# Two expert outputs per token joined to the residual by accumulating DMAs

## The chip, the cores and the metric

The kernel runs on one core of a Trainium2 chip. The metric is device time in microseconds for one execution. A core has five engines with queues of their own: PE (TensorE, matrix products), VectorE (DVE), ScalarE (ACT), GpSimd (POOL) and SyncE (SP), and 16 DMA engines which they share. Instructions of one queue run in order; between queues only semaphores order the work. A DMA raises its semaphore by 16 when all of its data has landed.

## What is computed

A model of two layers over 4 x 512 tokens of width 128. In layer 0 a gated recurrence and a mixture of 8 experts both read the normalised input and are added to it. The mixture picks two experts for each token and adds their weighted outputs:

```python
out = out * scores.reshape(-1, 1)
combined = out.reshape(N, TOP_K, h).sum(axis=1)      # TOP_K = 2
...
x = x + _L0_attn_ref(xn, ...) + _L0_ffn_ref(xn, ...)
xn = _layernorm(x, axis=-1)
x = x + _L1_attn_ref(xn, ...) + _L1_ffn_ref(xn, ...)
```

Layer 1 normalises the sum again and feeds a state-space scan and a mixture of 64 experts. Nothing of layer 1 can start before the sum of layer 0 is complete. The change is at this join.

## The kernel before

Tokens lie 128 to a tile, 16 tiles (NT), in 4 blocks (NB) of 4 tiles (TPB). The residual `res` is in SBUF as [128, 16, 128] float32: partition p, tile c holds token 128 c + p. It is loaded at L396.

Layer 0's experts work on tokens sorted by expert, in 39 tiles (NTILE) of 128 rows. In a loop over these tiles (PE from L1399, ScalarE from L729, VectorE from L1098, POOL from L530) a tile's rows are gathered from DRAM by an indirect DMA of POOL (`fetch`, L497), go through the expert and are scattered by another indirect DMA (`send`, L509) into the DRAM tensor `parts`. Each row of `parts` is one token's output of one of its two experts, 512 bytes, already weighted. Behind a padding area the rows lie by token, then by expert: row 2 t + k is expert k of token t. The attention's output is added to `res` on VectorE (L1081), one block at a time, within the same loop; the semaphore `back_dve` counts that chain.

The join comes after the loop:

- SP waits for the last of `back_dve` (L430) and for all scatters (`o_sent`, L432), then loads `parts` into the SBUF tensor `both` with four DMAs, one a block (L435). Each has its own semaphore `both_in[b]`. A token's two rows are adjacent, so a row of a transfer is 1 KB.
- VectorE (from L1109) waits for a block, adds both outputs to `res` (L1113, two instructions of 128 x 512), and takes the statistics for the normalisation (L1115 bn_stats, L1119 bn_aggr, four each). After the last block it forms the variance (L842), ScalarE takes the root (L754), VectorE inverts it (L1124) and normalises 16 tiles into `xn_tok` (L1126). PE transposes these (L1256), and layer 1 goes on from there.
- POOL, after its last scatter, splits the weights of the first two expert groups of layer 1 into high and low parts (`split_group`: L477, L478, L538), raises `g_split`, and then waits for ScalarE's exponentials (L546). PE uses these parts from L1486 and L1490 on.
- SP, after the loads, enters a loop that waits for `g_split` and reloads `g_raw` (L388) for the next two groups.

Layer 1 has accumulating DMAs of its own: POOL issues them at L572 and adds `state`, 512 KB with 4 KB in each partition, to `y_t` (the memory of `xn_tok`), both in SBUF.

Of the kernel before, what the change touches and what calls it, by code (L numbers as in the profile page):

```python
# [6 lines left out]
ALU = mybir.AluOpType  # L7
# [6 lines left out]
P = 128  # L14
# [24 lines left out]
def program(nc, x, wq, wk, wv, wa, wg, wo, rms_scale, wqkv, w1, w2, A_log, B_mat, C_mat, D_vec, W_dt, b_dt,  # L39
# [9 lines left out]
    NB, T, D = x.shape  # L49
    NTOK = NB * T  # L50
    NT = NTOK // P
    TPB = TB // P
    E0, F2, _ = w1.shape
    F = F2 // 2
    FT = [(s, min(P, F - s)) for s in range(0, F, P)]
    NF = len(FT)
    E1, _, H1 = rw1.shape
    GE = P // H1
    NG = E1 // GE
    NS = A_log.shape[1]  # L60
    ES, _, HS = sw1.shape
    NSH = ES * HS // P
    LN_EPS, RMS_EPS = 1e-5, 1e-6
    TOPK = 2
    NTILE = NTOK * TOPK // P + E0 - 1
    XRING, ORING, TRING, AHEAD = 12, 4, 3, 10
# [11 lines left out]
    parts = nc.dram_tensor("parts", (NTOK * TOPK + NTILE * P, D), F32).ap()  # L78

    with ExitStack() as ctx:  # L80
        def sb(name, shape, dt=F32):
            return ctx.enter_context(nc.sbuf_tensor(name, shape, dt))

        def sem(name):
            return ctx.enter_context(nc.semaphore(name))
# [25 lines left out]
        def over(base, limit):  # L111

            offset = base

            def place(name, shape, dt=F32):
                nonlocal offset
                t = nc.alloc_sbuf_tensor_at(name, shape, dt, offset=offset)
                offset += (math.prod(shape[1:]) * 4 + 31) // 32 * 32
                assert offset <= limit, (name, offset, limit)
                return t  # L120

            return place

        res = sb("res", [P, NT, P])
# [23 lines left out]
        both = over(base, nc.sbuf_base)("both", [P, NT, TOPK, P])  # L148
# [122 lines left out]
        h0_made, sil_ready, gated, h_turned = sem("h0_made"), sem("sil_ready"), sem("gated"), sem("h_turned")  # L271
        h_copied, o_made, o_out = sem("h_copied"), sem("o_made"), sem("o_out")
        o_sent = [sem(f"o_sent{r}") for r in range(ORING)]
        both_in = [sem(f"both_in{b}") for b in range(NB)]
        fr_pe, fr_act, fr_dve = sem("fr_pe"), sem("fr_act"), sem("fr_dve")
        back_pe, back_act, back_dve = sem("back_pe"), sem("back_act"), sem("back_dve")
        dt_made, dt_left, sp_exp, sp_log = sem("dt_made"), sem("dt_left"), sem("sp_exp"), sem("sp_log")
# [30 lines left out]
        def counted(steps, ops):  # L308

            table, total = {}, 0  # L310
            for name, b in steps:
                total += ops[name]
                table[name, b] = total
            return table
# [29 lines left out]
        def beside(n, names):  # L344

            return [(name, b) for b, first in enumerate(BACK_AT) for name in names if first + BACK_STEPS[name] == n]

        BK_DVE = counted([what for n in range(NTILE + 3) for what in beside(n, BACK_OPS)], BACK_OPS)
# [23 lines left out]
        def _(sp):  # L372
# [54 lines left out]
            sp.wait_ge(fr_dve, max(FR_DVE.values()))  # L427
            sp.dma_start(sw1_raw[:, :, :], sw1.rearrange("e d h -> d e h")).then_inc(late_in, 16)
            sp.dma_start(sw2_sb[:, :, :], sw2.rearrange("e (c h) d -> h (e c) d", h=P)).then_inc(late_in, 16)
            sp.wait_ge(back_dve, max(BK_DVE.values()))  # L430
            for r in range(ORING):
                sp.wait_ge(o_sent[r], 16 * ((NTILE - 1 - r) // ORING + 1))  # L432
            parts_v = parts[NTILE * P:NTILE * P + NTOK * TOPK, :].rearrange("(c p k) d -> p c (k d)", p=P, k=TOPK)
            for b in range(NB):
                sp.dma_start(both[:, b * TPB:(b + 1) * TPB, :, :].rearrange("p c k d -> p c (k d)"),  # L435
                             parts_v[:, b * TPB:(b + 1) * TPB, :]).then_inc(both_in[b], 16)
            with sp.Fori(0, NG // GPI - 1) as i:
                for j in range(GPI):

# [14 lines left out]
        def _(pool):  # L454
            own = Chain(pool, pool_own)
# [37 lines left out]
            def fetch(n):  # L493

                if n >= XRING:
                    pool.wait_ge(x_turned, n - XRING + 1)
                pool.indirect_dma_start(  # L497
                    out=x_tile[n % XRING][:, :], out_offset=None, in_=normed,
                    in_offset=bass.IndirectOffsetOnAxis(ap=token[:, n:n + 1], axis=0)).then_inc(x_tile_in[n % XRING], 16)
# [6 lines left out]
            def send(n):  # L506

                pool.wait_ge(o_out, n + 1)
                pool.indirect_dma_start(  # L509
                    out=parts, out_offset=bass.IndirectOffsetOnAxis(ap=part[:, n:n + 1], axis=0),  # L510
                    in_=t_out[n % ORING][:, :], in_offset=None).then_inc(o_sent[n % ORING], 16)

            def prepare(n):

                sel_v = sel[:, :].rearrange("p (c h) -> p c h", h=H1)
                if n == 27:
                    pool.wait_ge(late_in, 16 * 8)
                    split(rout_raw[:, :], rout_hi[:, :], rout_lo[:, :])
                    own(pool.tensor_tensor(ssm_cb[:, :], ssm_raw[:, 1, :], ssm_raw[:, 2, :], ALU.mult))
                if n == 29:  # L520
                    split(sw1_raw[:, :, :], sw1_hi[:, :, :], sw1_lo[:, :, :])
                    pool.nop().then_inc(weights_split, 1)
                if n == 31:
                    own(pool.memset(sel[:, :], 0.0))
                if n in (33, 35):
                    own(pool.affine_select(out=sel_v, in_=sel_v, compare_op=ALU.not_equal, fill=1.0,
                                           base=-E1 * ((n - 33) // 2), pattern=[[-1, E1], [0, H1]],
                                           channel_multiplier=1))

            for n in range(NTILE):  # L530
                send(n)
                prepare(n)
                if n + AHEAD < NTILE:
                    fetch(n + AHEAD)

            def split_group(j):
                split(g_raw1[j][:, :, :].rearrange("p e h -> p (e h)"), g_hi[j][:, :], g_lo[j][:, :])
                own(pool.tensor_copy(sel_now[j][:, :], sel[:, j * P:(j + 1) * P]))  # L538
                pool.nop().then_inc(g_split, 1)
# [10 lines left out]
            for b in range(POOL_LOGS):  # L550
                pool.wait_ge(sp_exp, b + 1)
                e, _, p = softplus_bufs[b]
                own(pool.tensor_scalar(p[:, :], e[:, :], -1.0 / 4, 1.0 / 3, ALU.mult, ALU.add))
                own(pool.tensor_tensor(p[:, :], p[:, :], e[:, :], ALU.mult))
                own(pool.tensor_scalar(p[:, :], p[:, :], 1.0, -1.0 / 2, ALU.mult, ALU.add))
                own(pool.tensor_tensor(p[:, :], p[:, :], e[:, :], ALU.mult))
                own(pool.tensor_scalar(p[:, :], p[:, :], 1.0, 1.0, ALU.mult, ALU.add))
                own(pool.tensor_tensor(p[:, :], p[:, :], e[:, :], ALU.mult))
                pool.nop().then_inc(sp_poly, 1)
# [268 lines left out]
        def _(dve):  # L828
            own = Chain(dve, dve_own)
# [52 lines left out]
            q, k, v = (qkv[:, :, n * E0:(n + 1) * E0] for n in range(3))  # L882
# [224 lines left out]

            dve.wait_ge(back_dve, max(BK_DVE.values()))
            for b in range(NBLK):  # L1109
                dve.wait_ge(both_in[b], 16)  # L1110
                r = res[:, b * TPB:(b + 1) * TPB, :]
                for k in range(TOPK):
                    own(dve.tensor_tensor(r, r, both[:, b * TPB:(b + 1) * TPB, k, :], ALU.add))  # L1113
                for t in range(b * TPB, (b + 1) * TPB):
                    dve.bn_stats(stats[:, t, :], res[:, t, :]).then_inc(dve_own, 1)  # L1115
                own.n += TPB
                own.wait()
                for t in range(b * TPB, (b + 1) * TPB):
                    dve.bn_aggr(mv[:, t, :], stats[:, t, :]).then_inc(dve_own, 1)  # L1119
                own.n += TPB  # L1120
# [65 lines left out]
            def poly(b):  # L1186

                e, _, p = softplus_bufs[b]
                dve.wait_ge(sp_exp, b + 1)
                own(dve.tensor_scalar(p[:, :], e[:, :], -1.0 / 4, None, ALU.mult))  # L1190
                for c in (1.0 / 3, -1.0 / 2, 1.0):
                    own(dve.scalar_tensor_tensor(p[:, :], p[:, :], c, e[:, :], ALU.add, ALU.mult))
# [31 lines left out]
            for i in range(NG // GPI):  # L1224
                c = i * GSTEPS
# [13 lines left out]
            for b in range(NBLK):  # L1239
                dve.wait_ge(sum_turned, b + 1)  # L1240
                r = res[:, b * TPB:(b + 1) * TPB, :].rearrange("p t d -> p (t d)")
# [306 lines left out]
```

## Time and profile before

| | us |
|---|---|
| median of 3 runs | 472.01 (471.5 to 472.09) |
| profiled execution | 475.62 |
| span of the profiled execution, first to last instruction | 473.9 |

| engine | busy us | share of the span |
|---|---|---|
| PE | 346.5 | 73% |
| VectorE | 347.8 | 73% |
| ScalarE | 261.5 | 55% |
| GpSimd | 243.2 | 51% |

Times in the rows are from the start of the span. A busy share is an average over stages with different limits, so the page is read together with the chain that ended last. That chain goes back from the last instruction, at each step to what released it. The join lies between 232 and 253 us.

### The profile page before, as it was taken

To read this page: it belongs to the slowest core of one execution; us is meant where nothing else is said; L and a number is where in the kernel's file an instruction comes from. 1 tells how busy PE (TensorE), PEld (TensorE's weight loads), DVE (VectorE), ACT (ScalarE), POOL (GpSimd) and SP (SyncE) were. 2 spreads that over 40 slices of the span, in tenths; PEclk is the share of its full clock that TensorE was granted. 3 is DMA by queue.
4 is the path that set the end of the run, shared out by engine and by line. 5 is a ranking of instruction groups with operands and counts; after the bars stand their busy time and mean duration, and the time that the engine had idled before them with its cause. 6 is when DMAs were issued, how large, how long until landed. Compare 5 with 4: busy or idle time off the path is not lost.

```text
span 473.9 us, 5780 instructions
## 1 busy us (share of the span) xinstructions
PE 346.5 (73%) x1491; PEld 247.2 (52%) x1491; DVE 347.8 (73%) x615; ACT 261.5 (55%) x440; POOL 243.2 (51%) x254
## 2 busy tenths in 40 slices
PE   1846879667975987779506848977887887887883
PEld 0435659356854866668403524544554554554542
DVE  5679998897864866648169759908688688688674
ACT  1477654546458346374505675355856856856820
POOL 3475300704763676776800049005577877877850
PEclk9977675959997898998956975997999999999997
DMA  6374100100111112120160000004658658668574
GB/s 175 94 200 128 25 1 1 45 11 24 46 39 29 34 41 81 43 42 21 35 190 0 0 0 2 0 0 89 126 101 161 123 116 163 122 119 162 112 152 111
DMA packets 36213, 35.09 MB, mean 74 GB/s; under 512 B 12166, under 2 KB 30839, under 8 KB 36183
## 3 DMA queue, kind: packets, MB, share of 16 engines
q0 software_dynamic: 7104, 21.90, 22.7%
q1 hardware_dynamic: 29078, 12.84, 10.2%
q8 instruction: 14, 0.23, 0.2%
q14 instruction: 17, 0.13, 0.1%
HBM read 13.29 MB, written 4.65 MB: 38 GB/s over the span
## 4 chain that ended last, share of the span: by engine, by line
PE 35%; POOL 19%; DVE 19%; issue 13%; ACT 6%; DMA 3%; another core or an unknown queue 2%; DVEq 1%; SPq 0%; POOLq 0%; ACTq 0%
POOL state L568 10%; PE psum L1376 5%; POOL xn_tok L572 4%; PE psum L1349 4%; POOL g_hi L581 3%; PE psum L1365 3%; PE psum L1389 3%; PE psum L1443 3%; PE psum L292 3%; PE psum L293 2%; PE psum L294 2%; PE psum L1352 2%; PE psum L1355 2%; PE psum L1338 1%
## 5 line engine op out<-in xcount | busy, mean ns | idle before, releaser
L1212 DVE TENSOR_TENSOR_SCAN state<-dec,win_t 128x1024 f32<-128x1024 f32 x32 | 73.4, 2293 | 26.5 <-ACT dec L777 26.5
L568 POOL TENSOR_SCALAR state<-state,ssm_cb 128x1024 f32<-128x1024 f32 x32 | 49.7, 1553 | 48.0 <-DVE state L1212 45.0
L812 ACT ACTIVATE sil<-psum,vec_t 128x512 f32<-128x512 f32 x64 | 43.2, 687 | 48.3 <-PE psum L294 37.7
L509 POOL DMA_INDIRECT parts<-t_out,part x39 | 41.0, 1050 | 48.3 <-ACT t_out L726 41.9
L1498 PE MATMUL psum<-hid,g_w 128*128 128x512 f32 x128 | 62.1, 599 | 0.0
L1221 DVE TENSOR_TENSOR hid<-sil,psum 128x512 f32<-128x512 f32 x64 | 41.7, 676 | 12.9 <-ACT sil L812 10.9
L497 POOL DMA_INDIRECT x_tile<-normed,token x39 | 41.3, 1059 | 13.4 <-issue 10.7
L292 PE MATMUL psum<-xn_hi,g_hi 128*128 128x512 f32 x64 | 39.7, 620 | 11.3 <-ACT sil L812 11.3
L1094 DVE TENSOR_TENSOR t_hid<-t_sil,psum 128x352 f32<-128x352 f32 x39 | 20.3, 521 | 32.3 <-ACT t_sil L710 23.5
L717 ACT ACTIVATE t_hid_t<-psum 128x384 f32<-128x384 f32 x39 | 19.2, 492 | 38.9 <-PE psum L1365 25.3
L1376 PE MATMUL psum<-w_out,t_hid_t 128*128 x234 | 37.5, 300 | 2.2 <-ACT t_out L726 1.4
L1490 PE MATMUL psum<-cw_hl,sel_now 128*128 128x512 f32 x64 | 26.9, 420 | 14.9 <-DVE hid L1221 14.9
L1376 PEld LDWEIGHTS psum<-w_out,t_hid_t 128*128 128x128 f32 x234 | 31.6, 205 | 5.3 <-issue 4.2
L572 POOL DMA_DIRECT2D xn_tok<-state x32 | 28.8, 899 | 10.2 <-POOL state L568 9.6
L1349 PE MATMUL psum<-w_hi,xt_hi 128*128 x78 | 25.1, 406 | 11.8 <-issue 11.8
L1498 PEld LDWEIGHTS psum<-hid,g_w 128*128 128x128 f32 x128 | 24.5, 191 | 15.0 <-issue 11.5
L777 ACT ACTIVATE dec<-dt_t,ssm_a 128x2044 f32<-128x2044 f32 x16 | 31.1, 1992 | 0.1
L292 PEld LDWEIGHTS psum<-xn_hi,g_hi 128*128 128x128 f32 x64 | 12.5, 195 | 26.4 <-ACT sil L812 19.3
L1338 PE MATMUL psum<-ident,x_tile 128*128 128x128 f32 x39 | 12.1, 310 | 18.8 <-DVE xt_lo L1086 13.7
L294 PE MATMUL psum<-xn_lo,g_hi 128*128 128x512 f32 x64 | 25.7, 402 | 0.0
L293 PE MATMUL psum<-xn_hi,g_lo 128*128 128x512 f32 x64 | 25.7, 402 | 0.0
L1490 PEld LDWEIGHTS psum<-cw_hl,sel_now 128*128 128x128 f32 x64 | 12.3, 193 | 22.3 <-DVE hid L1221 20.1
(308 smaller groups left out, 887.6 us busy)
## 6 DMA issues: line engine op xcount, KB each, us to landing
xn_tok<-state POOLq DMA_DIRECT2D x32, 512.0 KB, 4.5
e_raw<-in_L_ffn_w SPq DMA_DIRECT2D x16, 128.0 KB, 2.2
both<-parts SPq DMA_DIRECT2D x4, 512.0 KB, 5.6
e_raw<-in_L_ffn_w SPq DMA_DIRECT2D x8, 176.0 KB, 2.6
res<-in_L_attn_x SPq DMA_DIRECT2D x4, 256.0 KB, 3.8
normed<-rows SPq DMA_DIRECT2D x1, 1024.0 KB, 5.2
g_raw<-in_L_ffn_w SPq DMA_DIRECT2D x16, 64.0 KB, 2.3
g_w<-in_L_ffn_w SPq DMA_DIRECT2D x16, 64.0 KB, 2.2
```

Source lines behind the costliest of these rows:

```text
L292: pe.matmul(acc, w_hi, m_hi, start=True, stop=False)
L497: pool.indirect_dma_start(out=x_tile[n % XRING][:, :], out_offset=None, in_=normed, in_offset=bass.IndirectOffsetOnAxis(ap=token[:, n:n + ...
L509: pool.indirect_dma_start(out=parts, out_offset=bass.IndirectOffsetOnAxis(ap=part[:, n:n + 1], axis=0), in_=t_out[n % ORING][:, :], in_off ...
L568: own(pool.tensor_scalar(state[k][:, :], state[k][:, :], ssm_cb[:, i * GPI + k // 2:i * GPI + k // 2 + 1], 0.0, ALU.mult, ALU.add))
L572: pool.dma_start(y_t[:, (k % 2) * HALF:(k % 2 + 1) * HALF], state[k][:, :], accum_op=ALU.add).then_inc(y_in[k], 16)
L812: act.activation(sil[:, c % 2, :], ps[c % 2][:, :], ACT.Silu, bias=vec_t[:, V_B1 + c // NBLK:V_B1 + c // NBLK + 1]).then_inc(h_silu, 1)
L1212: dve.tensor_tensor_scan(state[k][:, :], dec[n % DECS][:, at_half], win_t[:, at_half], 0.0, ALU.mult, ALU.add).then_inc(scanned, 1)
L1221: dve.tensor_tensor(hid_ring[c % HRING], sil[:, c % 2, :], ps[2 + c % 2][:, :], ALU.mult).then_inc(hid_done, 1)
L1349: pe.matmul(acc[c], xt_hi[n % TRING][:, :], w_hi[:, e, half[c]].rearrange("p a f -> p (a f)"), start=True, stop=False)
L1376: ins = pe.matmul(ps[O_BANK][:, 0:P], t_hid_t[n % 2][:, c * P:(c + 1) * P], w_out[:, e, c, :].rearrange("p a d -> p (a d)"), start=(c == 0 ...
L1490: pe.matmul(ps[2 + c % 2][:, :], sel_now[j][:, :], blk(cw_hl, tb), start=True, stop=True).then_inc(cwx_made, 1)
L1498: pe.matmul(ps[4 + tb][:, :], g_w2[g % GPI][:, :], hid_ring[c % HRING], start=False, stop=g == NG - 1, skip_group_check=True).then_inc(g_o ...
```

## The change

The four loads of SP, the tensor `both` as their target and the eight additions of VectorE go. In their place POOL, after its last scatter, issues four DMAs that add into `res` as they write: first expert 0 for the first and the second half of the tiles, then expert 1 for each half. An expert 1 DMA waits until the expert 0 DMA of its half has landed. VectorE waits for both DMAs of the half in which a block lies, and takes the statistics.

```diff
--- before.py
+++ after.py
@@ -271,7 +271,7 @@
         h0_made, sil_ready, gated, h_turned = sem("h0_made"), sem("sil_ready"), sem("gated"), sem("h_turned")
         h_copied, o_made, o_out = sem("h_copied"), sem("o_made"), sem("o_out")
         o_sent = [sem(f"o_sent{r}") for r in range(ORING)]
-        both_in = [sem(f"both_in{b}") for b in range(NB)]
+        both_in = [sem(f"both_in{h}") for h in range(2)]
         fr_pe, fr_act, fr_dve = sem("fr_pe"), sem("fr_act"), sem("fr_dve")
         back_pe, back_act, back_dve = sem("back_pe"), sem("back_act"), sem("back_dve")
         dt_made, dt_left, sp_exp, sp_log = sem("dt_made"), sem("dt_left"), sem("sp_exp"), sem("sp_log")
@@ -427,13 +427,6 @@
             sp.wait_ge(fr_dve, max(FR_DVE.values()))
             sp.dma_start(sw1_raw[:, :, :], sw1.rearrange("e d h -> d e h")).then_inc(late_in, 16)
             sp.dma_start(sw2_sb[:, :, :], sw2.rearrange("e (c h) d -> h (e c) d", h=P)).then_inc(late_in, 16)
-            sp.wait_ge(back_dve, max(BK_DVE.values()))
-            for r in range(ORING):
-                sp.wait_ge(o_sent[r], 16 * ((NTILE - 1 - r) // ORING + 1))
-            parts_v = parts[NTILE * P:NTILE * P + NTOK * TOPK, :].rearrange("(c p k) d -> p c (k d)", p=P, k=TOPK)
-            for b in range(NB):
-                sp.dma_start(both[:, b * TPB:(b + 1) * TPB, :, :].rearrange("p c k d -> p c (k d)"),
-                             parts_v[:, b * TPB:(b + 1) * TPB, :]).then_inc(both_in[b], 16)
             with sp.Fori(0, NG // GPI - 1) as i:
                 for j in range(GPI):
 
@@ -533,6 +526,18 @@
                 if n + AHEAD < NTILE:
                     fetch(n + AHEAD)
 
+            pool.wait_ge(back_dve, max(BK_DVE.values()))
+            for r in range(ORING):
+                pool.wait_ge(o_sent[r], 16 * ((NTILE - 1 - r) // ORING + 1))
+            parts_v = parts[NTILE * P:NTILE * P + NTOK * TOPK, :].rearrange("(c p k) d -> p c k d", p=P, k=TOPK)
+            for k in range(TOPK):
+                for h in range(2):
+                    at_half = slice(h * NT // 2, (h + 1) * NT // 2)
+                    if k > 0:
+                        pool.wait_ge(both_in[h], 16 * k)
+                    pool.dma_start(res[:, at_half, :], parts_v[:, at_half, k, :], accum_op=ALU.add
+                                   ).then_inc(both_in[h], 16)
+
             def split_group(j):
                 split(g_raw1[j][:, :, :].rearrange("p e h -> p (e h)"), g_hi[j][:, :], g_lo[j][:, :])
                 own(pool.tensor_copy(sel_now[j][:, :], sel[:, j * P:(j + 1) * P]))
@@ -1107,10 +1112,7 @@
 
             dve.wait_ge(back_dve, max(BK_DVE.values()))
             for b in range(NBLK):
-                dve.wait_ge(both_in[b], 16)
-                r = res[:, b * TPB:(b + 1) * TPB, :]
-                for k in range(TOPK):
-                    own(dve.tensor_tensor(r, r, both[:, b * TPB:(b + 1) * TPB, k, :], ALU.add))
+                dve.wait_ge(both_in[b // 2], 16 * TOPK)
                 for t in range(b * TPB, (b + 1) * TPB):
                     dve.bn_stats(stats[:, t, :], res[:, t, :]).then_inc(dve_own, 1)
                 own.n += TPB
```

## Rows read from the trace of the kernel before

**Rows 1.** The page, part 4: shares of the span in the chain that ended last.

```profile
PE 35%; POOL 19%; DVE 19%; issue 13%; ACT 6%; DMA 3%; another core or an unknown queue 2%; DVEq 1%; SPq 0%; POOLq 0%; ACTq 0%
```

**Rows 2.** The chain in order of time at the join: start, us, what.

```profile
234.73 2.24 DMA parts<-t_out,part
...
237.13 3.98 DMA both<-parts
...
241.20 0.70 DVE res L1113
241.93 0.70 DVE res L1113
242.65 0.88 DVE stats L1115 x4
243.56 0.38 DVE mv L1119 x4
...
250.52 0.88 DVE stats L1115 x4
251.43 0.39 DVE mv L1119 x4
...
252.74 4.19 DVE xn_tok L1126 x16
```

**Rows 3.** Groups of instructions, 234 to 253 us: busy us, mean ns | idle before.

```profile
L1113 DVE TENSOR_TENSOR res<-res,both 128x512 f32<-128x512 f32 x8 | 5.4, 680 | 12.1 <-DMA both<-parts 12.0
L1115 DVE BATCH_NORM_STATS2 stats<-res 128x6 f32<-128x128 f32 x16 | 3.5, 280 | 0.1
...
L1119 DVE BATCH_NORM_AGGREGATE mv<-stats 128x2 f32<-128x6 f32 x16 | 1.5, 157 | 0.1
```

**Rows 4.** Line 435, the loads; then windows: start:end, us, five engines, clock, DMA, GB/s.

```profile
L435 SPq DMA_DIRECT2D both<-parts x4: 359/432/510, 237.1 to 238.9; - x4
...
DMA to landing us min/median/max: 4.0/5.6/7.3
...
2.50:5.50 3.00, 0.00 (x0) 0.00 (x0) 1.50 (x8) 0.00 (x0) 2.43 (x8) 1.00 1.02 288
...
242.50:244.00 1.50, 0.00 (x0) 0.00 (x0) 1.43 (x10) 0.00 (x0) 0.00 (x0) 0.50 1.07 366
```

**Rows 5.** Line 572, layer 1's accumulating DMAs: ns min/median/max; and a window of one.

```profile
L572 POOL DMA_DIRECT2D xn_tok<-state x32: 890/896/1002, 324.1 to 459.4; - x32
...
DMA to landing us min/median/max: 4.5/4.5/5.3
...
425.10:427.70 2.60, 2.60 (x7) 1.14 (x6) 1.68 (x1) 2.60 (x2) 2.30 (x3) 1.00 1.04 202
```

**Rows 6.** Timeline of POOL from the last scatter: start, us, instruction, idle before.

```profile
234.73 0.97 POOL L509 DMA_INDIRECT parts<-t_out,part  x1 [0.30 <-issue]
235.73 0.30 POOL L477 TENSOR_SCALAR g_hi<-g_raw 128x128 fp32r<-128x128 f32 x1
...
238.02 0.29 POOL L538 CAST sel_now<-sel 128x128 fp32r<-128x128 bf16 x1
```

**Rows 7.** Windows around the join: PE, PEld, DVE, ACT, POOL busy; clock; DMA share; GB/s.

```profile
237.00:241.00 4.00, 0.00 (x0) 0.00 (x0) 0.00 (x0) 0.00 (x0) 1.04 (x3) 0.50 0.67 203
...
253.00:257.00 4.00, 3.85 (x15) 2.74 (x16) 4.00 (x17) 3.44 (x7) 0.00 (x0) 0.50 0.00 0
257.00:261.00 4.00, 3.71 (x17) 1.82 (x17) 3.58 (x6) 2.07 (x4) 0.00 (x0) 0.96 0.00 0
```

**Rows 8.** Lines 1081, 1490, 583 (first and last start) and a wait of POOL.

```profile
L1081 DVE TENSOR_TENSOR res<-res,psum x4: 677/678/680, 130.7 to 226.2; 128x512 f32<-128x512 f32 x4
...
L1490 PEld LDWEIGHTS psum<-cw_hl,sel_now x64: 186/188/330, 314.8 to 457.0; 128*128 128x128 f32 x64
...
L583 POOL CAST sel_now<-sel x14: 289/291/291, 330.1 to 446.7; 128x128 fp32r<-128x128 bf16 x14
...
278.32 0.43 POOL L549 MEMSET dec<- 128x4 f32 x3 [40.01 <-ACTq L793]
```

## The prediction

> **What bounds the kernel now.** I read the page's share of the chain first. No engine owns this kernel: PE has 35% of the chain that ended last, POOL and VectorE 19% each [rows 1]. So totals of busy time say nothing here, and a change is worth what it does to the chain at its place. The next view is the same chain in order of time around that place [rows 2]. The last scatter of an expert output is issued at 234.73 and lands 2.24 us later. SP, released, issues the load of both at 237.13; the first quarter lands after 3.98 us. From 241.20 the chain stays on VectorE: two additions of 0.70 us, four statistics, four aggregates, four times over, until 251.8; then the root, and from 252.74 the 16 normalising instructions from which the whole second layer starts. Nothing else is on the way: the stretch is serial, and PE idles through it [rows 7]. A microsecond gained or lost before 251.8 moves the end of the kernel by a microsecond.
>
> The groups of that stretch [rows 3] say what VectorE does in it: eight additions, 5.4 us, and statistics and aggregates of 3.5 and 1.5 us. In the chain a block takes 2.65 us (10.6 / 4), of which 1.45 are its additions (241.20 to 242.65, [rows 2]); 1.2 us are left, and two blocks take 2.5.
>
> The stretch thus is: 237.1 to 241.2 for the transfer, 10.6 us of VectorE, end at 251.8. Of the four loads only the first shows; the other three land beneath the additions (to landing 4.0 to 7.3 us, the last issued at 238.9, [rows 4]).
>
> **Part 1: removed.** Four SP loads and eight additions. The additions are worth 5.4 us on the chain, and the first load 4.1 us. That is all there is to win: 9.5 us, out of which the new transfers have to be paid.
>
> **Part 2: added.** Four accumulating DMAs on POOL's queue, each half of the tokens (512 KB) and one of the two experts. POOL is ready for the first at about 237.2: the same landing at 236.97, which was SP's to wait for, and 0.3 us, the gap that POOL shows ahead of a DMA [rows 6]. Call D the time that POOL spends issuing one, and d the time that the DMA engines spend on the data of one.
>
> The nearest row is the accumulating DMA of the second layer, state into xn_tok: the same 512 KB, float32, SBUF to SBUF. It occupies POOL for 0.89 us and lands 4.5 us after its start [rows 5]. In a stretch where almost only one of them moves, the engines are full (share 1.04) and carry 202 GB/s [rows 5]: 524 KB in 2.6 us. So 4.5 = 0.9 of issue + 2.6 of data + 1.0 of start and completion. Two plain loads give the scale: with 1 KB rows full engines carry 366 GB/s, with 512 B rows 288 [rows 4]. An accumulation thus costs almost twice a copy.
>
> Two things differ from that row, and both come from the shape: parts is interleaved, so each DMA has 8 x 128 = 1024 rows of 512 B where state has 128 rows of 4 KB.
>
> d: the lower end is 2.6 us (row length free). Upper: if the loss from small rows counts for both the read and the add, 2.6 x (366/288) squared = 4.2, an estimate. I take one factor of 366/288, 3.3 us, since only one of the two sources has short rows by necessity. A gain is excluded only if an accumulation from HBM is no faster than one from SBUF; what it would be otherwise is rival A.
>
> D: lower end 0.9 us, the row. Upper end: if POOL's time is all per row, 8 x 0.9 = 7.2 us. Which? The scatter moves 128 rows of 512 B with an index for each and takes 0.97 us; the accumulation has an extra source for each of its 128 rows and takes 0.89 [rows 5, 6]. A second source that costs nothing visible speaks for a price that is mostly fixed. If half is per row, D is 4.0; if a fifth, 2.2. I take 2.5, nearer to the row.
>
> **The sum.** The order is k0 half 0, k0 half 1, k1 half 0, k1 half 1; a k1 is issued when its own k0 has landed. All share the same engines, so once they are fed the data are back to back: while D is under d, the next one is issued beneath the data of the one before. VectorE now needs both halves of the experts before a half's statistics; the first half's 2.5 us lie beneath the last transfer, the last half's 2.5 do not, and 0.1 is the release.
> End = 237.2 + D + 1.0 + 4 d + 2.6.
> With D = 2.5, d = 3.3: 237.2 + 2.5 + 1.0 + 13.2 + 2.6 = 256.5, against 251.8: 4.7 us later. With both lower ends (0.9, 2.6): 252.1, 0.3 us later. So even where the shape costs nothing, four accumulations one after the other (10.4 us of data) use up what the 5.4 us of additions and the overlapped loads gave. Break-even is D + 4 d = 11.0.
>
> The profiled execution took 475.6 us for a span of 473.9 and the median is 472.0; I add the difference to the median: 472.0 + 4.7 = 476.7.
>
> A price from the Trainium skill stands against this. *DMA: Bandwidth & Descriptors*, section "Anatomy of one DMA — SWDGE (gpsimd) path", gives a DMA issued from GpSimd as 2.0 us plus bytes over 436 GB/s, 3.2 us for 512 KB, where the row of this trace shows 4.5. The same section says that many descriptors can be generated before the cost of more shows. By that sentence D would be 0.9 and the sum 237.2 + 0.9 + 1.0 + 13.2 + 2.6 = 254.9, 3.1 us later; no row of this trace shows a DMA of POOL with more than 128 rows.
>
> **Part 3: moved.** SP's wait for back_dve goes to POOL: the last addition of the attention's output is done by 227 [rows 8], no cost. Both expert groups' splits (six instructions, 2.1 us, 235.73 to 238.3 [rows 6]) now stand behind the four DMAs on POOL, including two waits for landings, so they run at about 253 to 256. Who needs them: PE's first load of sel_now at 314.8 [rows 8], and SP's two reloads of g_raw, issued now after them, for a use at 330. POOL's own next work waits until 278 for the exponentials [rows 8]. The cover is at least 22 us, and it moves with the chain; cost nothing. If POOL's issues took all of the upper end they would end before 267, still covered. The reloads, which stood behind the four loads on SP's queue, no longer meet them.
>
> PE's clock: from 237 to 257 PE is granted 0.50, that is 1.2 GHz, having done nothing since 233; the next four microseconds show 0.96 [rows 7]. It works from 253.1 and is at 2.4 GHz by 257 to 261. A longer idle time leaves the same state at its end, so the slow stretch shifts and costs nothing more.
>
> **Rivals.**
> A, faster: an accumulation from HBM runs at the rate of a plain load. For: one source is HBM and no longer the SBUF; the two reads might overlap. Against: the row of 202 GB/s at full engines. Price: d = 524/288 = 1.8. k0 half 0 lands at 240.9, k1 half 0 is issued at 241.2 and lands 3.7 later, 244.9; its k1 half 1 follows within 2 us, and both statistics run from 244.9 to 249.9: 1.9 us earlier, 470.1. It decides from about d = 2.5, 210 GB/s. By the skill's 3.2 us for each DMA the same chain would end at 249.0, 469.2; this trace speaks against it with 4.5.
>
> B, issue bound: POOL pays per row and D passes d. Then the end is 237.2 + 4 D + 1.0 + d + 2.6. D = 4: 8.3 later, 480.3. D = 5: 264.1, 12.3 later, 484.3. D = 7.2: 272.9, 493. For: every DMA of POOL here has 128 rows, so nothing bounds the slope. Against: the scatter and accumulation pair above.
>
> C, small rows weigh on an accumulation more than on a copy, since each then stands for two reads and a write: d = 4.6, an estimate between the second and the third power of 366/288 (4.2 and 5.3). D = 2.5: 237.2 + 2.5 + 1.0 + 18.4 + 2.6 = 261.7, 9.9 later, 481.9.
>
> E, nothing: the ends meet, the result within 0.9 us. For: both lower ends give +0.3.
>
> **How the numbers follow.** The forecast (D from 0.9 to 3.7, d from 2.6 to 3.6) has 0.50 and an own range of 473 to 480; A 0.13; B 0.17; C 0.12; E 0.08. A difference of 0.2%, 0.9 us, is about what can be told from none. Faster by more: A, 0.13. Same: E and a sliver of the forecast, 0.12. Slower: 0.75. The range goes from 470.9, which takes in a part of A, to 487, which takes in C and B up to D = 5.7; outside stay most of A and the top of B, under 0.2.
>
> **What would show it.** In the changed kernel the four DMAs' own rows: their time on POOL (D: 2.5 forecast, 0.9 the row, over 4 is B), the spacing of their landings, the GB/s at full engines (160 forecast, 202 the row, 290 is A, under 120 is C). VectorE's wait before the first statistics should end near 250.6 (253.9 less 3.3), and the last half's near 254. The normalising instructions should start near 257.4. From there to the end, both traces should run in step; if POOL's splits or g_raw's reloads show as a releaser of anything, part 3 is wrong. The prediction is wrong if D + 4 d is under 11 or the issue is the longer of the two.

## The result and the profile after

The changed kernel takes 476.73 us (median of 5 runs, 476.42 to 480.08) where the kernel before takes 472.09 (471.5 to 475.7). The ratio is 1.0086, 95% interval 1.0044 to 1.0128: slower by 4.1 us, clear of no change. Measured once more beside the experiments, it was 1.0116 (1.0068 to 1.0164). The forecast was 4.7 us.

| | before | after |
|---|---|---|
| profiled execution | 475.62 us | 480.08 us |
| its span | 473.9 us | 478.3 us |
| VectorE busy | 347.8 us | 341.8 us |
| GpSimd busy | 243.2 us | 251.0 us |

The engine that the change relieves is busy for 6 us less, and the kernel is slower. The page shows what the DMA engines got in exchange: the same 35.09 MB in over 2000 packets more. The packets of POOL's queue, q0, take 26.0% of the engines' span where they took 22.7%.

```profile
span 478.3 us, 5772 instructions
DMA packets 38260, 35.09 MB, mean 73 GB/s; under 512 B 12165, under 2 KB 32886, under 8 KB 38230
q0 software_dynamic: 11264, 23.99, 26.0%
```

The chain in order of time at the join, to be laid beside [rows 2] (start, us, what):

```profile
235.91 2.23 DMA parts<-t_out,part
...
238.84 1.00 POOL res L538
239.84 8.53 DMA res<-parts
...
248.65 6.99 DMA res<-parts
...
255.66 0.89 DVE stats L1117 x4
256.57 0.38 DVE mv L1121 x4
256.95 0.77 DVE stats L1117 x4
257.74 0.39 DVE mv L1121 x4
...
258.25 0.19 DVE nrm L847
```

Where the chain before had one short transfer and then VectorE's work, it now has 17 us from POOL's first issue to the last landing, and VectorE has only the tail. The measure that I use from here on is the stretch from the landing of the last scatter to the start of the variance (L842, now L847). Before it is 236.97 to 251.94, 15.0 us; after, 238.14 to 258.25, 20.1 us.

The four DMAs' own rows (source line: ns min/median/max on POOL, then to landing), to be laid beside those of state in [rows 5]:

```profile
L538 POOL DMA_DIRECT2D res<-parts x4: 1551/1637/2338, 238.8 to 248.7; - x4
its engine sat idle before it (us, times) until:
  DMA res<-parts: 4.9, 2
  DMA parts<-t_out,part: 2.0, 1
...
DMA to landing us min/median/max: 6.4/6.8/8.5
```

And windows of the same stretch (the columns are those of [rows 7]):

```profile
238.84:241.20 2.36, 0.00 (x0) 0.00 (x0) 0.00 (x0) 0.00 (x0) 2.36 (x2) 0.50 0.00 0
...
247.50:249.50 2.00, 0.00 (x0) 0.00 (x0) 0.00 (x0) 0.00 (x0) 1.21 (x2) 0.50 0.59 68
249.00:255.00 6.00, 0.00 (x0) 0.00 (x0) 2.10 (x13) 0.00 (x0) 3.32 (x7) 0.50 1.38 172
```

There is nothing on the DMA engines for 2.36 us from the first issue; full engines carry 172 GB/s, so 524 KB take 3.05 us; and between the second and the third DMA the engines are half empty.

Outside the stretch the two profiled executions differ as well. The last scatter landed 1.2 us later in the changed kernel, and from the variance to the end it took 220.05 us (478.3 - 258.25) where before took 221.96. With the stretch's 5.1 that makes the 4.4 us between the spans (1.2 + 5.1 - 1.9). Over all fourteen executions profiled here, of kernels that are the same up to the last scatter or have small edits ahead of it, that landing lies between 233.8 and 239.5 us, and the rest after the variance takes 220.0 to 223.4. So a single execution's time says little about a microsecond; the stretch is steady (20.11 and 20.02 in two executions of the changed kernel), and I judge the mechanisms by it and the kernels by their ratios.

### The profile page after: what moved, and what is told of

It is laid out like the page before. It is cut to its first block, busy times and chain, and to the rows that moved or that the text cites. A ratio compares the mean times of both kernels' runs of the same rounds, so it can differ in the third digit from the quotient of the medians.

```text
span 478.3 us, 5772 instructions
## 1 busy us (share of the span) xinstructions
PE 345.4 (72%) x1491; PEld 247.8 (52%) x1491; DVE 341.8 (71%) x607; ACT 261.6 (55%) x440; POOL 251.0 (52%) x258
## 2 busy tenths in 40 slices
DMA packets 38260, 35.09 MB, mean 73 GB/s; under 512 B 12165, under 2 KB 32886, under 8 KB 38230
## 3 DMA queue, kind: packets, MB, share of 16 engines
q0 software_dynamic: 11264, 23.99, 26.0%
## 4 chain that ended last, share of the span: by engine, by line
PE 34%; POOL 21%; DVE 17%; issue 13%; ACT 6%; DMA 6%; another core or an unknown queue 1%; DVEq 0%; POOLq 0%; SPq 0%; ACTq 0%
POOL state L573 11%; PE psum L1378 6%; POOL xn_tok L577 4%; PE psum L1351 4%; POOL g_hi L586 4%; DMA res<-parts 3%; PE psum L1391 3%; PE psum L1445 3%; PE psum L1367 3%; PE psum L1354 2%; PE psum L1357 2%; PE psum L292 2%; PE psum L294 2%; PE psum L293 2%; POOL g_lo L587 1%
## 5 line engine op out<-in xcount | busy, mean ns | idle before, releaser
L573 POOL TENSOR_SCALAR state<-state,ssm_cb 128x1024 f32<-128x1024 f32 x32 | 52.4, 1638 | 43.8 <-DVE state L1214 40.9
L502 POOL DMA_INDIRECT parts<-t_out,part x39 | 39.7, 1018 | 51.9 <-ACT t_out L731 46.9
L490 POOL DMA_INDIRECT x_tile<-normed,token x39 | 41.0, 1052 | 13.3 <-issue 11.3
L1258 PE MATMUL psum<-ident,xn_tok 128*128 128x128 f32 x32 | 7.0, 400 | 25.4 <-DVE xn_tok L1128 25.4
```

The costliest lines, as they stand in the source:

```text
L490: pool.indirect_dma_start(out=x_tile[n % XRING][:, :], out_offset=None, in_=normed, in_offset=bass.IndirectOffsetOnAxis(ap=token[:, n:n + ...
L502: pool.indirect_dma_start(out=parts, out_offset=bass.IndirectOffsetOnAxis(ap=part[:, n:n + 1], axis=0), in_=t_out[n % ORING][:, :], in_off ...
L573: own(pool.tensor_scalar(state[k][:, :], state[k][:, :], ssm_cb[:, i * GPI + k // 2:i * GPI + k // 2 + 1], 0.0, ALU.mult, ALU.add))
```

## The experiments

All stretches, in us, each from one profiled execution, with the ratio to the kernel before on the same chip:

| kernel | stretch | ratio (95%) |
|---|---|---|
| before | 14.97 | 1 |
| after, after_again | 20.11, 20.02 | 1.0086, 1.0116 (1.0068 to 1.0164) |
| plain_copies | 15.91 | 1.0030 (0.9992 to 1.0069) |
| long_rows | 17.09 | 1.0075 (1.0040 to 1.0111) |
| by_block | 18.21 | 1.0078 (1.0046 to 1.0111) |
| long_by_block | 17.08 | 1.0069 (1.0029 to 1.0109) |
| own_targets | 21.24 | 1.0179 (1.0122 to 1.0237) |
| own_targets_clear | 20.57 | 1.0186 (1.0145 to 1.0228) |
| splits_first | 21.24 | 1.0116 (1.0075 to 1.0156) |
| before_long_rows | 15.01 | 1.0017 (0.9984 to 1.0051) |
| pool_helps, once more | 13.52, 13.47 | 0.9986 (0.9961 to 1.0011), 1.0012 (0.9976 to 1.0047) |
| pool_helps_long | 14.62 | 0.9984 (0.9945 to 1.0023) |

**The changed kernel again.**

> The changed kernel itself, beside the others. By the stretch from the landing of the last scatter to the variance (15.0 us before, 20.1 after in the profiled executions), every theory expects 20 us again and 4.5 to 5.5 us over the kernel before. If the kernel's time differs by clearly less or more than the stretch does, something after the join moved too.

Stretch 20.0; the ratio of 1.0116 on 475.1 us is 5.5 us. The stretch (5.1) and the time agree; the loss is at the join.

**Copies in place of accumulations.**

```diff
-                    pool.dma_start(res[:, at_half, :], parts_v[:, at_half, k, :], accum_op=ALU.add
+                    pool.dma_start(flat_both[:, k, at_half, :], parts_v[:, at_half, k, :]
```

> The four DMAs of POOL with the same rows and waits, but as plain copies into the tensor both; the experts' outputs are left out of the sum. Second-read theory: 1.6 to 1.8 us of data each in place of 3.0, the stretch 15 to 15.5. Row theory: POOL's issue stays at 1.6 us and the start stays late, data about 2.6, the stretch 18 or more.

Stretch 15.9: 4.2 us of the 5.1 are gone, with the same rows, the same queue, the same waits. The row theory's 18 is out; the second-read theory's 15 to 15.5 is missed by 0.4. The lines are (source line of plain_copies, its chain, a window with full engines, then its page's q0):

```profile
L539 POOL DMA_DIRECT2D both<-parts x4: 882/904/957, 238.8 to 245.7; - x4
...
DMA to landing us min/median/max: 4.9/5.2/5.6
...
238.79 4.92 DMA both<-parts
...
244.00 4.97 DMA both<-parts
...
242.00:243.00 1.00, 0.00 (x0) 0.00 (x0) 0.00 (x0) 0.00 (x0) 0.00 (x0) 0.50 1.09 336
...
q0 software_dynamic: 7680, 23.99, 24.3%
```

Four things are read here. Full engines carry 336 GB/s of these copies (299 from 247 to 248), not far from twice the 172 of the accumulations. POOL issues 1024 rows as plain copies in 0.90 us, and as accumulations in 1.64. And for the same 23.99 MB the queue has 7680 packets where the accumulations have 11264. The difference of 3584 is 4096 - 512: the four DMAs have 4096 rows, which as accumulations go one to a packet of 512 B, and as copies eight to a packet of 4 KB. And the chain that is left is two landings one after the other, 4.9 and 5.0 us, and then VectorE's statistics of all four blocks, 4.8 us, since the first half's expert 1 lands only at 248.97.

**Long rows.**

```diff
-own(pool.iota(numbers[:, 0:NT], [[P * TOPK, NT]], base=NTILE * P + k, channel_multiplier=TOPK))
+own(pool.iota(numbers[:, 0:NT], [[1, NT]], base=NTILE * P + k * NTOK, channel_multiplier=NT))
...
-parts_v = parts[...].rearrange("(c p k) d -> p c k d", p=P, k=TOPK)
+parts_v = parts[...].rearrange("(k p c) d -> p k (c d)", p=P, k=TOPK)
```

> The changed kernel with a token's outputs numbered so that the rows of one expert and one half are 4 KB in each partition (the store of the normalised tokens and the gather's indices are renumbered with them). Row theory (the 512 B rows make the issue and the data dear): the stretch falls from 20.1 to 15 or less, the kernel to no more than before. Second-read theory (an accumulation reads two places, and that is most of the price): issue 0.9 us, data 2.6 us each as in layer 1, together about 3 us off, the stretch stays near 17, 1.5 to 2 us over before. Serial theory (expert 1 waits behind expert 0, the engines stand idle): 1 us at most.

Stretch 17.1, as the second-read theory had it, 2.1 us over before. Source line, and a window with full engines:

```profile
L538 POOL DMA_DIRECT2D res<-parts x4: 857/929/1297, 238.9 to 247.2; - x4
...
DMA to landing us min/median/max: 5.2/5.5/7.3
...
247.00:252.00 5.00, 0.00 (x0) 0.00 (x0) 1.98 (x12) 0.00 (x0) 2.98 (x7) 0.50 1.02 189
```

POOL's issue falls from 1.64 to 0.93 and the rate rises only from 172 to 189 GB/s. So the rows cost 3.0 us of the stretch. The number of packets alone does not make an accumulation slow: this kernel's page has 7680 of them on q0, as plain_copies has, and full engines still carry 189 GB/s where the copies had 299 to 336. How the 2.1 us that are left over before divide between the accumulation and the order of the four DMAs is not shown: copies with long rows were not tried. Nor is the second read itself: the sizes agree with it, but q0 has the same 23.99 MB with accumulations and with copies. In the ratio the 3.0 us do not show (1.0075 against 1.0086 and 1.0116).

**Without the wait between the experts.**

```diff
-                    if k > 0:
-                        pool.wait_ge(both_in[h], 16 * k)
-                    pool.dma_start(res[:, at_half, :], parts_v[:, at_half, k, :], accum_op=ALU.add
-                                   ).then_inc(both_in[h], 16)
+                    pool.dma_start(res[:, at_half, :] if k == 0 else aside[:, at_half, :], ..., accum_op=ALU.add
+                                   ).then_inc(both_in[h + 2 * k], 16)
```

> Expert 1 is added onto an idle tensor in place of the residual, so that its DMAs need not wait for those of expert 0; expert 1 is left out of the sum. Serial theory: the wait costs most of the loss, the stretch falls by 3 us or more. Theories of the data: only the gap of about 1 us between the second and the third DMA goes, the stretch near 19.

All theories missed this: 21.2, a microsecond longer. The next experiment takes SP's reloads of `g_raw` out of the way:

```diff
+            for n in range(4):
+                pool.wait_ge(both_in[n], 16)
             for j in range(GPI):
                 pool.wait_ge(g_in[j], 16)
                 split_group(j)
```

> As own_targets, but POOL splits the expert weights only when all four DMAs have landed, so that SP's reloads of g_raw cannot run beside them; expert 1 is left out of the sum. If those reloads made the last DMA late there, the stretch falls from 21.2 to about 19 us (four times 3.0 of data, no gap). If the four accumulations in one queue are slow in themselves, it stays above 20.5.

20.6, over the bound of 20.5 that I had set, by little. Its source line and windows:

```profile
L537 POOL DMA_DIRECT2D w_out<-parts x2: 2987/3335/3683, 240.3 to 241.2; - x2
...
250.00:253.00 3.00, 0.00 (x0) 0.00 (x0) 0.22 (x2) 0.00 (x0) 0.00 (x0) 0.50 1.40 175
253.00:254.00 1.00, 0.00 (x0) 0.00 (x0) 0.96 (x9) 0.00 (x0) 0.00 (x0) 0.50 0.42 52
254.00:255.00 1.00, 0.00 (x0) 0.00 (x0) 0.97 (x8) 0.00 (x0) 0.00 (x0) 0.50 0.24 30
```

The gap is gone, but POOL needs 3.0 and 3.7 us for the third and the fourth issue, the rate does not rise, and for the last two microseconds before the landing at 255.54 the engines are mostly empty (shares 0.42 and 0.24), at 52 and 30 GB/s. Taking the wait between the experts out thus gains nothing; what a wait costs by itself these two kernels do not show, since queuing four accumulations has a price of its own. Why the engines end so unevenly then is open; 0.7 us between the two kernels may be the reloads, but it is one execution against one. Their ratios are 8.5 and 8.8 us over before, 2 to 3 us more than their stretches explain (6.3 and 5.6); that is open too.

**Eight DMAs.**

```diff
-                for h in range(2):
-                    at_half = slice(h * NT // 2, (h + 1) * NT // 2)
+                for h in range(NB):
+                    at_half = slice(h * TPB, (h + 1) * TPB)
```

> The changed kernel with eight DMAs, one for each block and expert, with the same waits. VectorE's tail behind the last landing is one block, 1.3 us, in place of 2.5; the data are the same. Data theory: the stretch falls by the 1.2 us of the tail and the gap, to 18 to 19. Issue theory: POOL pays 0.9 us or more for each of eight, the first transfer starts earlier, and the stretch lies within 1 us of 20.1.

Stretch 18.2, 1.9 us less. POOL's row for 512 rows a DMA:

```profile
L538 POOL DMA_DIRECT2D res<-parts x8: 1274/1368/2988, 240.2 to 250.1; - x8
```

The eight issues fill POOL from 240.2 to 251.4. With 128 rows an accumulation's issue takes 0.86 (long_rows, shortest), with 512 rows 1.27, with 1024 rows 1.55: some 0.75 us and 0.5 to 1.1 ns a row. Even so the finer cut is worth more than it costs: the tail behind the last landing is one block, 1.2 us less, and that landing comes 0.7 us earlier in the stretch, since the rate no longer drops between the experts (157 to 187 GB/s in every microsecond from 245 to 255). The ratio, 1.0078, cannot be told from that of the changed kernel.

**Both.** The diffs are those two, on one kernel.

> Both of the edits that shortened the changed kernel's stretch: rows of 2 KB in each partition, and eight DMAs, one for each block and expert. If the gains are independent (3.0 from the rows, 1.9 from the blocks), the stretch is 15.2 and the kernel within 1 us of before. If POOL's fixed share of the issue takes over with eight DMAs, it is 16 or more. In neither case is it under 14.5: the data of two reads for 2 MB stay.

17.1: the gains do not add, and not because of POOL's fixed share. With long rows POOL waits for landings again (idle 3.6 us for four of them), and the chain is the accumulations' time to land:

```profile
L538 POOL DMA_DIRECT2D res<-parts x8: 857/930/1949, 240.1 to 250.0; - x8
its engine sat idle before it (us, times) until:
  DMA res<-parts: 3.6, 4
```

**POOL's splits ahead of the DMAs.**

```diff
+            for j in range(GPI):
+                pool.wait_ge(g_in[j], 16)
+                split_group(j)
             pool.wait_ge(back_dve, max(BK_DVE.values()))
```

> The changed kernel with POOL's two splits of expert weights where they were, ahead of the DMAs. The prediction held that moving them behind the DMAs costs nothing. Ahead of them they take 2.6 us from the end of the last scatter's issue, 1.3 us more than its landing needs: the first DMA starts 0.5 to 1.3 us later, and SP's reloads then run beside the accumulations. The stretch grows to 21 or 22. If it is 20 or less, the move was not free.

Stretch 21.2, 1.1 to 1.2 more (the landing is taken 2.24 us after the last scatter's issue at 235.13, as in the others). POOL's timeline:

```profile
238.44 0.29 POOL L531 CAST sel_now<-sel 128x128 fp32r<-128x128 bf16 x1
239.55 3.36 POOL L547 DMA_DIRECT2D res<-parts  x2 [0.82 <-POOL sel_now L531]
```

The first DMA starts 2.2 us after the landing in place of 0.7. The move of the splits behind the DMAs was free, and right: ahead of them they would have held the DMAs up. In the ratio it does not show (1.0116, as after_again).

**The other direction: the kernel before, improved.** Two edits on it, and both together. The first stands on POOL's queue behind the two splits.

```diff
+            for b in (2, 3):
+                pool.wait_ge(both_in[b], 16)
+                two = both[:, b * TPB:(b + 1) * TPB, :, :]
+                own(pool.tensor_tensor(two[:, :, 0, :], two[:, :, 0, :], two[:, :, 1, :], ALU.add))
+                pool.nop().then_inc(paired, 1)
...
-                for k in range(TOPK):
+                for k in range(1 if b in HELPED else TOPK):
```

> The kernel before, with POOL adding the two expert outputs of blocks 2 and 3 to each other while VectorE works on blocks 0 and 1; VectorE then needs one addition for each of those blocks. By the rows of before VectorE saves 2 x 0.7 = 1.4 us of the chain, and POOL's two additions of about 1.3 us are done before VectorE comes to them: the stretch 13.5, the kernel 1.4 us faster. If the two engines disturb each other, VectorE's additions grow and the gain is under 0.7.

> pool_helps once more, for its interval: its stretch was 1.4 us shorter than before, its time 0.3 us less and not separable. If the 1.4 us reach the end, the ratio is 0.997. If POOL's additions meet VectorE's in time, as they did in pool_helps_long, where one addition took 1.64 us in place of 0.69, the stretch is 14.5 in that execution.

The stretch is 13.5 both times, as forecast. The ratios are 0.9986 and 1.0012, both with 1 in the interval: 1.5 us in the stretch could not be shown at the end. (The 0.997 that they would be lies in the first interval and just outside the second.)

```diff
-own(pool.iota(numbers[:, 0:NT], [[P * TOPK, NT]], base=NTILE * P + k, channel_multiplier=TOPK))
+own(pool.iota(numbers[:, 0:NT], [[TOPK, NT]], base=NTILE * P + k, channel_multiplier=TOPK * NT))
...
-parts_v = parts[...].rearrange("(c p k) d -> p c (k d)", p=P, k=TOPK)
+parts_v = parts[...].rearrange("(p c k) d -> p (c k d)", p=P, k=TOPK)
```

> The kernel before, with tokens numbered so that the four loads into the tensor both have rows of 4 KB in place of 1 KB. Their full-engine rate was already 366 GB/s, and VectorE is the bound from the first landing on, so only the first load counts: 0 to 0.4 us off its 4.0 us, the stretch 14.6 to 15.0. If the row length mattered as much as it did for the accumulations (3 us of 20), the stretch would fall to 13.

15.0: no change. The loads after the first lie beneath VectorE's work, and the first takes 4.03 us where it took 3.98. The length of rows is worth 3 us of the stretch for the accumulations, which are the chain, and nothing for loads of which three in four are beneath VectorE's work.

> Both edits: the long rows, and POOL adding the two outputs of blocks 2 and 3 to each other. In pool_helps the second half's data landed late (POOL began at 245.5) and VectorE waited 0.3 us for it. With long rows that wait should go: the stretch 12.8 to 13.3, the kernel 1.5 to 2 us faster than before, and clear of it. If the loads do not land earlier, it is 13.5 as pool_helps.

14.6, against the forecast of 12.8 to 13.3. The loads did land earlier, so POOL's additions began at 241.1, and met VectorE's. Timeline of POOL, then of VectorE:

```profile
241.13 1.49 POOL L549 TENSOR_TENSOR both<-both 128x512 f32<-128x512 f32 x1 [5.98 <-DMA both<-parts]
...
240.84 2.33 DVE L1122 TENSOR_TENSOR res<-res,both 128x512 f32<-128x512 f32 x2
```

Two additions of 0.69 us took 2.33. In pool_helps POOL began at 245.5, beneath VectorE's statistics, and its first addition took 1.26. Its second began at 246.89 together with one of VectorE's; there POOL's took 1.79 and VectorE's the usual 0.69. No kernel beat the one before by a measurable amount.

## Why the prediction was right

The sign held, and so did the mechanism in the main: the accumulations, one after the other, cost more than the additions and the first load gave. The size is right in part by luck: 4.7 us forecast, 4.1 and 5.5 measured, 5.1 in the stretch, but its terms were off by up to 1.5 us, some up and some down, and one step, the data back to back, was wrong. The terms one by one, from the last scatter's landing (236.97 in the forecast, 238.14 in the trace) to that of the last accumulation (253.9 and 255.64):

- **What is won.** VectorE lost its eight additions (busy 6.0 us less) and its tail behind the last landing is 2.5 us (255.66 to 258.13), as worked out.
- **The start.** POOL issued 0.7 us after the landing, not 0.3. The chain shows the waits themselves with hundredths of a microsecond; 0.55 us are time in which POOL waits for nothing that the profile shows.
- **D.** 1.64 us in the median, not 2.5; nearer to the lower end than I had put it. Rival B, the issue as the bound, is out: 1.64 is under d, and between 128 rows and 1024 the shortest issue grows by only 0.7 us (0.86 to 1.55). The sentence of the Trainium skill (*DMA: Bandwidth & Descriptors*, "Anatomy of one DMA — SWDGE (gpsimd) path") that many descriptors can be generated before it shows agrees with plain_copies, 0.90 us for 1024 rows, and not with the accumulations, 1.64.
- **Start and completion.** 1.0 forecast. The engines are empty for 2.36 us from the first issue, of which 1.6 is D, and a landing follows the data by a fraction of a microsecond (empty engines from 248.1, landing at 248.37). With 0.5 for that, an estimate, it is 1.3.
- **d.** 3.3 forecast, 3.05 measured (172 GB/s). The factor 366/288 for the rows was too much: from long_rows (189) to the changed kernel the loss is 10%. Rival C is out with it.
- **Back to back.** This step was wrong. I held that each issue lies beneath the data of the one before. But an expert 1 DMA is issued only at its expert 0's landing, and with 0.3 + 1.6 + 0.8 us from there to its first data the engines emptied: 68 GB/s from 247.5 to 249.5. The first half's statistics show it too: they began 14.7 us after the scatter's landing (252.83), where 250.6 was forecast, 13.6. Of 17.5 us, 12.2 (4 x 3.05) are data at the full rate; some 1.5 are this gap and the slower edges. My 13.2 for the data was too high by 1.0 and the gap was missing: these two errors, and the high D against the late start, almost cancel. That is the luck in the number.

Together: forecast 0.2 + 2.5 + 1.0 + 13.2 = 16.9; measured 0.7 + 1.6 + 1.3 + 12.2 + 1.5 = 17.3 to the landing, which the trace has at 17.5.

**Rival A** had copies' speed for accumulations. plain_copies shows what it would have been worth: 15.9 in place of 20.1. But even that is 0.9 us over before, and A forecast 1.9 us under. A's price was too kind by the late start (0.4) and, twice in its chain, by the time to land: 4.9 and 5.0 us where it had 3.7. So A's gain could not have come even at the rate of copies. The 3.2 us that the Trainium skill gives for a DMA of this size (same page and section) is not what a copy took here either: 4.9 to 5.6, though each of these had another beside it.

**Part 3** held. The splits ran at 249.6 to 252.8, earlier than the 253 to 256 forecast; PE's first use of them was at 320.5, and splits_first shows that the other order costs 1.1 to 1.2 us of the stretch. PE's clock behaved much as said: in every window of the stretch above it is 0.50 after as before. In the second four microseconds behind the first normalising instruction it is 0.92 (263.32 to 267.32) where the kernel before had 0.96, in one execution each.

What is left unexplained is own_targets: without the wait there should have been 1 us to gain and there was 0.5 to 1.1 to lose.

## What to carry to other kernels

An accumulating DMA is not a free addition: it ran at 172 to 189 GB/s here where loads ran at 288 to 366 and copies of the same rows on the same queue at 299 to 336, and this kernel makes two onto the same place follow each other. Where it replaces a load that was overlapped with the additions, compare the whole serial path (issue, start, data, landing) with the exposed part of what it replaces, not with the engine's busy time. If it must be, give it long rows (3 us of 20 in the stretch here, not separable in the ratio); and if the experts' outputs can be loaded in blocks, let the additions run beneath the later loads, as the kernel before did.

## What the runs showed of the hardware that was not expected

- An accumulating DMA with 512 B rows sent one row to a packet, a plain one of POOL eight (11264 and 7680 packets on q0 for the same 23.99 MB), and its issue took 1.64 us against 0.90.
- Four accumulations queued without waits took no less time than with them (20.6 and 21.2 against 20.1 us); the third and fourth issue took 3.0 and 3.7 us, and the engines ended unevenly.
- Additions of two SBUF operands on POOL and VectorE at the same time hold each other up: 2.33 us for two of VectorE's that take 1.4 alone. In pool_helps two additions that began together took 1.79 on POOL and 0.69 on VectorE, so there only POOL's was held up. POOL's addition beside VectorE's statistics took 1.26 and did not slow them.
